# Statistics of two groups taken ahead, in a fused feed-forward / attention / feed-forward kernel

## The reference

```
x = x + 0.5 * ffn(layernorm(x))
x = x + attention(layernorm(x))       # 16 heads of 8, linear attention with rotary embedding
x = x + 0.5 * ffn(layernorm(x))       # the same weights as the first

layernorm(x) = (x - mean) / sqrt(var + 1e-5)     # over the 128 numbers, no scale or shift

ffn(x):  probs = sigmoid(x @ router.T)           # 8 experts
         the two best, their weights divided by their sum
         h = square(relu(x @ W1[e]))             # widths 4 x 128 and 4 x 256
         out = sum over the two chosen e of weight * (h @ W2[e])
```

## Time and profile before

| | |
|---|---|
| median of three executions | 792.01 us (791.9 to 795.37) |
| profiled execution, time | 793.06 us |
| profiled execution, span from first to last instruction | 791.3 us |
| mean granted TensorE clock | 0.993 of full speed |
| PE busy | 729.2 us (92%) |
| POOL busy | 686.2 us (87%) |
| ACT busy | 597.5 us (76%) |
| DVE busy | 581.6 us (74%) |

### The profile page before, as it was taken

The page is one execution under the profiler, slowest core; times in us unless marked ns, Lnnn a source line. Parts: engine busy times, 40 slices in busy tenths (PEclk is TensorE's granted clock), DMA queues, the critical chain, the costliest instruction groups (busy, mean ns, idle before and its releaser), DMA issues.

```text
span 791.3 us, 13302 instructions
## 1 busy us (share of the span) xinstructions
PE 729.2 (92%) x3736; PEld 594.3 (75%) x3736; DVE 581.6 (74%) x1832; ACT 597.5 (76%) x1220; POOL 686.2 (87%) x668
## 2 busy tenths in 40 slices
PE   6688788889999999999999999999999998989887
PEld 6466566667888888888888888888887877767665
DVE  3456788877879787877878797878777678676543
ACT  4577677668887978888888879788878766766765
POOL 3778867859999999999999999999999877666876
PEclk9999999989999999999999999999999999999999
DMA  5654113023233222233333332213333403303330
GB/s 181 187 163 133 37 72 107 2 107 108 108 109 121 91 91 69 99 110 108 121 109 120 109 122 84 79 68 112 116 108 121 122 2 107 110 13 121 121 121 27
DMA packets 31160, 79.38 MB, mean 100 GB/s; under 512 B 3312, under 2 KB 14448, under 8 KB 31088
## 3 DMA queue, kind: packets, MB, share of 16 engines
q1 hardware_dynamic: 30800, 78.47, 29.9%
q10 hardware_dynamic: 288, 0.07, 0.0%
HBM read 73.81 MB, written 4.72 MB: 99 GB/s over the span
## 4 chain that ended last, share of the span: by engine, by line
PE 27%; DVE 27%; POOL 18%; issue 13%; ACT 10%; DMA 4%; DVEq 1%; POOLq 0%; ACTq 0%; SPq 0%
POOL h_lo L880 9%; DVE hid L1047 7%; POOL root_f L874 4%; PE bank L509 4%; PE bank L529 3%; PE bank L511 3%; PE bank L510 3%; PE bank L531 3%; PE bank L530 3%; DMA g_all_f<-rows_f 3%; ACT h_hi L751 3%; DVE pick_f L1025 2%; ACT hid L740 2%; POOL x_lo_at L868 2%; ACT xn_f L697 2%
## 5 line engine op out<-in xcount | busy, mean ns | idle before, releaser
L880 POOL TENSOR_TENSOR h_lo<-hid,h_hi 128x512 fp32r<-128x512 f32 x384 | 492.8, 1308 | 70.0 <-ACT h_hi L751 69.4
L1047 DVE SCALAR_TENSOR_TENSOR hid<-bank,g_all_f 128x512 f32<-128x512 f32 x384 | 262.2, 684 | 137.8 <-PE bank L511 90.9
L740 ACT ACTIVATE hid<-hid 128x512 f32<-128x512 f32 x384 | 228.8, 622 | 50.0 <-DVE hid L1047 49.7
L751 ACT ACTIVATE h_hi<-hid 128x512 fp32r<-128x512 f32 x384 | 225.8, 620 | 4.9 <-PE bank L531 0.4
L509 PE MATMUL bank<-x_hi_f,w_hi 128*128 128x512 f32 x384 | 164.3, 428 | 16.1 <-DVE hid L1047 16.1
L529 PE MATMUL bank<-h_hi,w_hi 128*128 128x512 f32 x384 | 154.5, 402 | 12.5 <-POOL h_lo L880 12.5
L531 PE MATMUL bank<-h_hi,w_lo 128*128 128x512 f32 x384 | 152.6, 397 | 0.0
L511 PE MATMUL bank<-x_hi_f,w_lo 128*128 128x512 f32 x384 | 151.9, 396 | 0.0
L530 PE MATMUL bank<-h_lo,w_hi 128*128 128x512 f32 x384 | 151.9, 396 | 0.0
L510 PE MATMUL bank<-x_lo_f,w_hi 128*128 128x512 f32 x384 | 151.5, 395 | 0.0
L509 PEld LDWEIGHTS bank<-x_hi_f,w_hi 128*128 128x128 f32 x384 | 73.1, 190 | 40.7 <-DVE hid L1047 25.2
(11 more groups left out here) (105 smaller groups left out, 1045.2 us busy)
## 6 DMA issues: line engine op xcount, KB each, us to landing
g_all_f<-rows_f SPq DMA_DIRECT2D x128, 512.0 KB, 5.8
x_sb<-in_x SPq DMA_DIRECT2D x16, 256.0 KB, 3.3
out_x<-x_sb SPq DMA_DIRECT2D x16, 256.0 KB, 7.1
g_all_f<-in_w SPq DMA_DIRECT2D x2, 768.0 KB, 6.6
con<-in_const SPq DMA_DIRECT2D x1, 584.0 KB, 6.1
rows_f<-g_row_f SPq DMA_DIRECT2D x32, 16.0 KB, 1.4
g_all_f<-in_wqkv SPq DMA_DIRECT2D x1, 192.0 KB, 6.5
con<-in_const ACTq DMA_DIRECT2D x1, 68.0 KB, 3.2
```

The lines of the kernel that those rows point to most:

```text
L740: fn(h, h, ACT.Square).then_inc(s_sq[s], 1)
L751: fn(h_hi[:, c, :], hid[:, c % STAGE, :], ACT.Copy).then_inc(s_hhi[s], 1)
L880: gp.tensor_tensor(h_lo[:, c, :], hid[:, c % STAGE, :], h_hi[:, c, :].bitcast(F32), ALU.subtract).then_inc(s_hlo[s], 1)
L1047: v.scalar_tensor_tensor(hid[:, c % STAGE, :], hp[c % 2][:], 0.0, g_all[s][:, EXPERT[c], :], ALU.max, ALU.mult).then_inc(s_z[s], 1)
```

## The change

For groups 2 and 3 of `f1` the statistics are no longer taken in iterations -1 and 0. DVE takes them in iteration -2, behind `g_tok` of group 0 and ahead of the splitting of the attention weights (`stats_ahead`: eight `bn_stats`, eight `bn_aggr`). POOL computes both groups' inverse deviation and shift in four instructions of 8 columns instead of two times four instructions of 4 columns, at the end of iteration -2, behind `w_lo` (`inv_std_ahead`). Both write tiles of their own, and ACT's `norm` reads those for these two groups. ACT's place for `norm` stays. The three constant tiles become 8 columns wide.

```
+AHEAD_FROM, AHEAD = 2, 2
+        bn_ahead, mv_ahead = sb("bn_ahead", [P, AHEAD * TG, 6]), sb("mv_ahead", [P, AHEAD * TG, 2])
+        ve_ahead, nm_ahead, rstd_ahead, nbias_ahead = (
+            sb(n, [P, AHEAD * TG]) for n in ("ve_ahead", "nm_ahead", "rstd_ahead", "nbias_ahead"))
+        def ahead(s, n):
+            return s == "f1" and AHEAD_FROM <= n < AHEAD_FROM + AHEAD
...
         # norm, ACT
+                shift, scale, first = nbias[s], rstd[s], 0
+                if ahead(s, n):
+                    shift, scale, first = nbias_ahead, rstd_ahead, (n - AHEAD_FROM) * TG
...
         # inv_std on POOL; stats and mean_variance on DVE
-                if not live(n):
+                if not live(n) or ahead(s, n):
...
+            def inv_std_ahead():
+                last = AHEAD_FROM + AHEAD
+                pool.wait_ge(s_mv["f1"], last)
+                gp.tensor_tensor(ve_ahead[:], mv_ahead[:, :, 1], c_eps[:], ALU.add).then_inc(s_ve["f1"], AHEAD)
+                gp.tensor_tensor(nm_ahead[:], mv_ahead[:, :, 0], c_mone[:], ALU.mult).then_inc(s_ve["f1"], AHEAD)
+                pool.wait_ge(s_ve["f1"], last * 2)
+                gp.tensor_tensor(rstd_ahead[:], ve_ahead[:], c_mhalf[:], ALU.pow).then_inc(s_rstd["f1"], AHEAD)
+                pool.wait_ge(s_rstd["f1"], last)
+                gp.tensor_tensor(nbias_ahead[:], nm_ahead[:], rstd_ahead[:], ALU.mult).then_inc(s_nb["f1"], AHEAD)
...
         # end of POOL's iteration -2
                     gp.tensor_tensor(w2_lo[:], w2_raw.rearrange("p (c d) -> p c d", c=NC),
                                      w2_hi[:].bitcast(F32), ALU.subtract).then_inc(s_w2lo, 1)
+                    inv_std_ahead()
...
+            def stats_ahead():
+                for n in range(AHEAD_FROM, AHEAD_FROM + AHEAD):
+                    dve.wait_ge(s_load[n % 2], n * 8 + (16 - 8 * (n % 2)))
+                    for k in range(TG):
+                        i = v.bn_stats(bn_ahead[:, (n - AHEAD_FROM) * TG + k, :], x_sb[:, n * TG + k, :])
+                    i.then_inc(s_bn["f1"], 1)
+                for n in range(AHEAD_FROM, AHEAD_FROM + AHEAD):
+                    dve.wait_ge(s_bn["f1"], n + 1)
+                    for k in range((n - AHEAD_FROM) * TG, (n - AHEAD_FROM + 1) * TG):
+                        i = v.bn_aggr(mv_ahead[:, k, :], bn_ahead[:, k, :])
+                    i.then_inc(s_mv["f1"], 1)
...
         # DVE's iteration
                 spread_roots("f1", n1, 1)
+                if first_time(True, t + 2):
+                    stats_ahead()
                 weighted(t, 14)
```

More of the change, by code:

```diff
@@ L215, in build @@
         nbias = {s: sb(f"nbias_{s}", [P, TG]) for s in STREAMS}
-        c_eps, c_mhalf, c_mone = sb("c_eps", [P, TG]), sb("c_mhalf", [P, TG]), sb("c_mone", [P, TG])
+        c_eps, c_mhalf, c_mone = (sb(n, [P, AHEAD * TG]) for n in ("c_eps", "c_mhalf", "c_mone"))
+        bn_ahead, mv_ahead = sb("bn_ahead", [P, AHEAD * TG, 6]), sb("mv_ahead", [P, AHEAD * TG, 2])
+        ve_ahead, nm_ahead, rstd_ahead, nbias_ahead = (
+            sb(n, [P, AHEAD * TG]) for n in ("ve_ahead", "nm_ahead", "rstd_ahead", "nbias_ahead"))
         ex = {s: sb(f"ex_{s}", [P, TG, EXP]) for s in FFN}
@@ L694, in norm @@
                     act.wait_ge(s_t[s], value(n))
+                shift, scale, first = nbias[s], rstd[s], 0
+                if ahead(s, n):
+                    shift, scale, first = nbias_ahead, rstd_ahead, (n - AHEAD_FROM) * TG
                 for k in range(TG):
                     tile = x_sb[:, bass.ds(value(n * TG + k), 1), :].rearrange("p a d -> p (a d)")
-                    i = fn(xn[s][:, k, :], tile, ACT.Identity, bias=nbias[s][:, k:k + 1], scale=rstd[s][:, k:k + 1])
+                    i = fn(xn[s][:, k, :], tile, ACT.Identity, bias=shift[:, first + k:first + k + 1],
+                           scale=scale[:, first + k:first + k + 1])
                 i.then_inc(s_xn[s], 1)
@@ L790, in _ @@
             act.wait_ge(s_pconst, 1)
-            fn(spare[:], c_mone[:], ACT.Exp)
+            fn(spare[:], c_mone[:, 0:TG], ACT.Exp)
             def iteration(t, par):
@@ L851, in inv_std @@
             def inv_std(s, n):
-                if not live(n):
+                if not live(n) or ahead(s, n):
                     return
                 pool.wait_ge(s_mv[s], value(n + 1))
-                gp.tensor_tensor(ve[s][:], mv[s][:, :, 1], c_eps[:], ALU.add).then_inc(s_ve[s], 1)
-                gp.tensor_tensor(nm[s][:], mv[s][:, :, 0], c_mone[:], ALU.mult).then_inc(s_ve[s], 1)
+                gp.tensor_tensor(ve[s][:], mv[s][:, :, 1], c_eps[:, 0:TG], ALU.add).then_inc(s_ve[s], 1)
+                gp.tensor_tensor(nm[s][:], mv[s][:, :, 0], c_mone[:, 0:TG], ALU.mult).then_inc(s_ve[s], 1)
                 pool.wait_ge(s_ve[s], value(n * 2 + 2))
-                gp.tensor_tensor(rstd[s][:], ve[s][:], c_mhalf[:], ALU.pow).then_inc(s_rstd[s], 1)
+                gp.tensor_tensor(rstd[s][:], ve[s][:], c_mhalf[:, 0:TG], ALU.pow).then_inc(s_rstd[s], 1)
                 pool.wait_ge(s_rstd[s], value(n + 1))
                 gp.tensor_tensor(nbias[s][:], nm[s][:], rstd[s][:], ALU.mult).then_inc(s_nb[s], 1)
+            def inv_std_ahead():
[7 more added lines that the diff above has]
+                gp.tensor_tensor(nbias_ahead[:], nm_ahead[:], rstd_ahead[:], ALU.mult).then_inc(s_nb["f1"], AHEAD)
             def low_part(s, n, par):
```

## The result

Over 22 executions of each kernel the changed one took 789.93 us (788.07 to 791.76), the one before 792.12 us (788.48 to 795.45). The ratio is 0.997, with a 95% interval of 0.9959 to 0.998: 2.4 us less, between 1.6 and 3.2. The forecast was 789.2 us, 2.8 less than before. The profiled execution after took 789.24 us with a span of 787.5, 3.8 less than the span before.

What follows compares the result with a forecast made beforehand. It took a ring of waits between g_all transfers, not the fullest engine, as the bound in iterations -1 and 0. Terms -2.8 +0 +0 give 790.3 by the profiled execution, median 789.2 us; 8 in 10 range 786.3 to 792.8.

Steps and rivals of the forecast that it cites:

- The ring: Iterations -1 and 0: a loop of waits from one g_all landing to the next, 23.4 and 24.2 us, sets the time.
- 2 x 1.4 us: Iterations -1 and 0: ACT's norm no longer waits for POOL's nbias, saving 1.4 us in each, 2.8 us together.
- It moves as a block: After 73.6 us everything waits on engines or transfers they release, and starts 2.8 us earlier together.
- The rival of a new phase, to either side: Rest of run: pick and cw meet POOL idle more often, 787.0 us (0.18), or busy more often, 794.7 with five (0.12).
- DVE's added work hidden: Iteration -2: 2.4 us of statistics, splitting ends at 24.7, before c0 at 26.05; 1.3 us in hand, cost zero.
- POOL's added work hidden: Iteration -2: the 8-column set takes 2.25 us, 23.59 to 25.8, before x_lo at 27.16; 1.3 us in hand.
- `cw` held: Iteration -1: DVE's cw waits for POOL's c1 remainder until 31.45; c4 is 0.3 us later, hidden with 0.4 in hand.
- The port rule: DVE and POOL share SBUF ports, locked for a whole instruction; DVE's last difference would end at 26.3, gain 2.6 us.
- the listed signs: What the profile after should show: times of added work, c0, norm, c3's remainder, g_all landings and the nbias wait.
- the remainder of c3: Iteration -1, POOL: starts at 33.8 instead of 35.22, because ACT rounds c3 1.4 us earlier.
- the wait for `nbias` in iteration 1: ACT in iteration 1: the same wait for nbias as before, since for groups 4 and later nothing changes.
- the held instruction: Iteration -2, DVE: the first splitting cast is held by POOL's w_lo until about 23.6 us.

Runs made afterwards that it cites:

- e1: Changed kernel with only group 2 taken ahead, group 3 keeping its statistics and POOL set in iteration 0; 790.99 us, ratio 0.9981 to the kernel before.
- e6: Kernel before with one more 4-column power on POOL between rstd and nbias in the sets of groups 2 and 3; 793.84 us, ratio 1.0027.
- e2: Changed kernel with POOL kept busy by four unused 4-column instructions at the old place in iterations -1 and 0; 789.34 us, ratio 0.9963 to before.
- e7: Changed kernel with the four splitting instructions of the attention weights put ahead of the statistics on DVE; 788.87 us in one run.
- e3: Kernel before with ACT's norm of f1 behind c5 instead of c2 in all iterations, nothing taken ahead; 790.02 us, ratio 0.996.
- e8: Changed kernel with two POOL sets of 4-column instructions at the end of iteration -2 instead of one of 8 columns; 790.35 us in one run.
- e9: Changed kernel with 28 transposes in PE's gap before the first attention product in iteration 1; 787.96 us, ratio 0.9951 to before.
- e10: Kernel before with 28 transposes in PE's gap before the first attention product in iteration 1; 790.59 us, ratio 0.998.

## Why the prediction was right

- *The ring, not the fullest engine.* Right. e1 takes the wait away in one iteration, e6 makes it longer without moving anything else, e2 takes it away with POOL as busy as before, and the stretch follows it each time.
- *2 x 1.4 us.* The stretches give 12.08 - 10.62 = 1.46 and 12.59 - 11.17 = 1.42, 2.88 in all. In the changed kernel's own profile the first is 1.33, since c2 had to wait for the second piece of `g_all` (27.24). The runs say 2.4 (1.6 to 3.2): forecast 2.8, inside. The median came out at 789.93, forecast 789.2. The difference of 0.4 in the gain is within the noise; part of it may be the hold on DVE in quick starts (up to 0.4), which was not separated.
- *It moves as a block.* Right, against the profile of the kernel before that is without those accidents. Ends of `pick`, second profile before against changed: 61.9 and 59.1, 86.8 and 84.0, 117.3 and 114.4, 455.0 and 451.9, 755.8 and 752.8. The lead is 2.8 to 3.2 us at every `pick` from iteration 0 to the end. The rival of a new phase, to either side, did not occur: the 32 `pick`s have a median of 0.75 us and a longest of 1.30 in both.
- *DVE's added work hidden.* Right in its end (24.7 forecast, 24.46 measured). The casts got in ahead of `w_lo` and the third instruction was the held one, not the first. The cover was not 1.3 us but none, because the first `g_all` usually lands near 24.5, not at 26.05: I took its landing from a single execution.
- *POOL's added work hidden.* Right, with a smaller margin. 2.25 us became 2.7, of which DVE's last difference is 0.2 (in e7, without it, 2.5), and `x_lo` followed at once. The slack in front of c3 covered it.
- *`cw` held.* It took 0.38 and 0.83 us instead of 0.17, and c4 was ready for ACT in both iterations, as expected.
- *The port rule.* In "SBUF — State Buffer", section "SBUF: two separate sides", of the Trainium skill the lock holds for the whole instruction. The trace agrees for `w_lo` (3.44 us of hold). For POOL's power it does not: in iteration 0 of e1 `cw` at 52.42 again took 0.17 us in the middle of a power (51.90 to 52.91). The rows decide. The changed kernel itself does not test it, since its last difference had ended at 24.46, before the power began at 24.67.

Of the listed signs these came: the statistics from 18.15 to 20.33, no idle time of ACT in front of `norm` in iterations -1 and 0, the remainder of c3 7.83 us behind c0 (forecast 7.75), and the wait for `nbias` in iteration 1 as before (1.31 and 1.33 us). These did not: the held instruction was another one, POOL's power ended at 26.31 and not before 25.8, c0 started at 24.61 and not at 26.05, and the second and third `g_all` were there at 46.64 and 68.98 instead of 48.05 and 70.8. Of the last two 1.4 us are the first transfer, which was quick by luck and not by the change.

## What to carry to other kernels

A small step that nobody needs soon can sit on the critical path only by its place in an engine's written order. Ask of every wait of an engine in a ring not how busy the releaser is but what stands behind the waiting instruction. Moving the waiting instruction to where its engine idles anyway (e3, over four iterations) was worth as much as computing its input earlier (over two), and both together more. Before a difference of a few microseconds is read off two profiles, profile the kernel before twice, and compare stretches between two events that depend on each other.

## What was not expected of the hardware

- The first transfer of 16 KB took 1.40 us in most profiles, but 3.11 in the first profile of the kernel before, whose second has 1.40, and 3.39 in e8. In the kernel before everything behind it shifted by 1.5 us.
- PE's idle gap of 3.47 us in iteration 1 was followed by the full clock in one profile and by 0.54 in the next profile of the same kernel, which cost 1.1 us. With the gap filled the clock behind it was 1.00 both times, but in e9 it fell to 0.55 behind the next gap, of 2.02 us, and in e10 it did not.
- A DVE difference of two SBUF tiles that takes 0.29 us alone was held 3.44 us beside POOL's `w_lo`. The statistics were not held: in e7 the last of the eight `bn_stats` and all `bn_aggr` ran beside `w_lo` (from 20.18 us) and took 1.64 and 0.62 us in all, as in the changed kernel, where they ran ahead of it.
